# Self-attention with two of its weight products made once on chip, and the key squares summed on ScalarE

## The reference, cut to what matters

```
x1 = layernorm(x + self_attention(x))
x2 = layernorm(x1 + cross_attention(x1, ctx))
y  = layernorm(x2 + mixture_of_experts(x2))

self_attention(x):                      # one head, 256 wide, causal
    n = (x - mean) / sqrt(var + 1e-5) * gamma + beta
    q, k, v = n @ qkv[:, :256], n @ qkv[:, 256:512], n @ qkv[:, 512:]
    p = softmax(mask(q @ k.T / 16))
    return (p @ v) @ o_proj + x

cross_attention: 16 query heads of 128, 4 key heads; q = n @ Wq + bq, k = ctx @ Wk + bk, each head
    divided by its root mean square (rmsnorm: mean(k*k) over 128, eps 1e-6) before the scores
```

## Time and profile before

| | us |
|---|---|
| median of 3 executions | 1892.0 (1889.64 to 1893.38) |
| the profiled execution, its own time | 1891.63 |
| span of that profile | 1889.9 |
| attention phase in that span | 0 to about 1158 |
| granted TensorE clock over the span | 0.925 of full speed |

### The profile page before, as it was taken

The page is one execution under the profiler, slowest core; times in us unless marked ns, Lnnn a source line. Parts: engine busy times, 40 slices in busy tenths (PEclk is TensorE's granted clock), DMA queues, the critical chain, the costliest instruction groups (busy, mean ns, idle before and its releaser), DMA issues. The chain is left out here.

```text
span 1889.9 us, 34753 instructions
## 1 busy us (share of the span) xinstructions
PE 1547.4 (82%) x9744; PEld 1255.8 (66%) x9744; DVE 1265.1 (67%) x3827; ACT 688.6 (36%) x1526; POOL 1050.4 (56%) x1023
## 2 busy tenths in 40 slices
PE   4799998999899898989999864777777878787685
PEld 3687877778788787777878753555555656555453
DVE  3688877877778887888888844345555555433486
ACT  3344444343443343434344411222232222222353
POOL 3457666666566666666666742445555545555321
PEclk7799999999999999999999976889999898988799
DMA  7323231222212111121111295655565655554496
GB/s 244 118 91 104 73 106 62 94 82 89 89 62 95 63 59 67 45 75 47 66 59 52 81 277 157 182 165 160 162 182 161 181 160 172 172 167 129 169 417 278
DMA packets 182979, 246.41 MB, mean 130 GB/s; under 512 B 30972, under 2 KB 159561, under 8 KB 178388
## 3 DMA queue, kind: packets, MB, share of 16 engines
q1 hardware_dynamic: 149188, 169.71, 28.7%
q0 software_dynamic: 27648, 69.28, 10.0%
q10 hardware_dynamic: 6032, 6.13, 0.9%
HBM read 136.19 MB, written 117.19 MB: 134 GB/s over the span
## 5 line engine op out<-in xcount | busy, mean ns | idle before, releaser
L1555 POOL DMA_INDIRECT expert_out_scratch<-y,target x320 | 318.7, 996 | 296.6 <-DVE y L1779 196.0
L558 POOL DMA_INDIRECT slot_scratch<-xrow x256 | 258.7, 1010 | 188.6 <-DVE xrow L1174 117.1
L598 PE MATMUL bank_c<-wq_w,x1t 128*128 128x512 f32 x768 | 215.4, 433 | 62.9 <-DVE q_work L1016 53.7
L598 PEld LDWEIGHTS bank_c<-wq_w,x1t 128*128 128x128 f32 x768 | 154.6, 209 | 113.1 <-DVE q_work L1016 67.8
L1614 PE MATMUL bank_g<-gu,x_turned 128*128 (+1 forms) x1408 | 217.1, 303 | 14.9 <-issue 12.4
L503 POOL TENSOR_TENSOR q_rs<-q_ve,minus_half 128x8 f32<-128x8 f32 x64 | 137.4, 2147 | 146.6 <-DVE q_ve L1005 142.9
L1614 PEld LDWEIGHTS bank_g<-gu,x_turned 128*128 128x128 f32 x1408 | 194.4, 214 | 31.0 <-issue 30.5
L1633 PE MATMUL bank_y<-dp,inter_t 64*128 (+1 forms) x352 | 137.2, 473 | 85.2 <-DVE y L1779 60.0
L1671 ACT ACTIVATE x_turned<-bank_x 128x512 f32<-128x512 f32 x176 | 105.3, 598 | 272.8 <-PE bank_x L1596 161.1
L1770 DVE TENSOR_TENSOR inter<-silu,bank_g 128x128 f32<-128x128 f32 x176 | 50.2, 285 | 220.1 <-ACT silu L1678 144.7
L744 PE MATMUL bank_d<-wo_w,o2t 128*128 128x256 f32 x1536 | 194.5, 287 | 2.0 <-DVE o2t L933 2.0
(11 more groups left out here) (240 smaller groups left out, 3305.3 us busy)
## 6 DMA issues: line engine op xcount, KB each, us to landing
x_rows<-slot_scratch SPq DMA_DIRECT2D x320, 136.0 KB
results<-expert_out_scratch SPq DMA_DIRECT2D x32, 1024.0 KB, 10.1
slot_scratch<-zeros SPq DMA_DIRECT2D x16, 816.0 KB, 4.2
dp<-in_down SPq DMA_DIRECT2D x161, 64.0 KB
slot_scratch<-zeros SPq DMA_DIRECT2D x8, 1088.0 KB, 9.4
gu<-in_gate_up SPq DMA_DIRECT2D x11, 768.0 KB
expert_out_scratch<-y,target POOLq DMA_INDIRECT x320
token_row_scratch<-xrow SPq DMA_DIRECT2D x32, 136.0 KB
```

Of the source, the lines that this page charges most:

```text
L558: nc.gpsimd.indirect_dma_start(out=slot_d[:, :], out_offset=bass.IndirectOffsetOnAxis(ap=xrow[slot][:, SLOT8 + k:SLOT8 + k + 1].bitcast(U3 ...
L598: last = nc.tensor.matmul(target, left[a][:, c, :], right(b, c), start=(n == 0 and c == 0), stop=(n == len(PASSES) - 1 and c == C - 1))
L1555: nc.gpsimd.indirect_dma_start(out=y_d[:, :], out_offset=bass.IndirectOffsetOnAxis(ap=target[n % 8][:, j:j + 1], axis=0), in_=y[s % 4][:, ...
```

## The change

Once, ahead of the loop (`fuse`), PE turns the three parts of qkv, multiplies Wq Wk^T and Wv Wo (the last with a factor 0.5), and the two products take the place of qkv in the three-pass format, 512 columns instead of 768. ACT issues its DMAs first, o_proj ahead of them, and then copies for `fuse`. Per tile, one product gives t = n Wq Wk^T and v' = 0.5 n Wv Wo. Only t is turned; the scores are t against the full-precision x_n turned, for which ACT keeps one more copy (xn_full). The exponentials are used undivided; p @ v' is one matmul that yields the output rows, and the reciprocal of the row sum comes in at `x1_add`. As v' is halved, x_res is added once and the layernorm's eps is LN_EPS / 4. `self_output`, `copy_v`, `copy_self_out` and p1n are gone. The key squares move from POOL to ACT, one Square per head with the engine's own row sum, and wait also for the key transposes of the tile before. Two waits of SP ahead of the last weight loads and the places of some tiles in memory are also changed. The order of DVE's step is not edited: the logits copy stands where it stood, in `route_choose` after `x_moments`.

```
@@ tensors
-        qkv_w = [sb(f"qkv_w{n}", [P, C, 3 * D], F32R) for n in (HI, LO)]
-        x_g, x_n, v = (sb(name, [P, D]) for name in ("x_g", "x_n", "v"))
+        qkv_w = [sb(f"qkv_w{n}", [P, C, 2 * D], F32R) for n in (HI, LO)]
+        x_g, x_n = (sb(name, [P, D]) for name in ("x_g", "x_n"))
         qk = sb("qk", [P, 2 * D])
+        v = qk[:, D:2 * D]
...
@@ SP
-                sp.wait_ge(sig["v_projected"], TILES)
-                sp.wait_ge(sig["q_projected"], 4 * TILES)
+                sp.wait_ge(sig["self_proj"], TILES)
+                sp.wait_ge(sig["q_biased"], 4 * TILES)
...
-                sp.wait_ge(sig["q_transposed"], 2 * TILES)
-                sp.wait_ge(sig["k_transposed"], TILES)
+                sp.wait_ge(sig["scored"], 2 * TILES)
@@ POOL
-            def square_keys(t):
-                pool.wait_ge(sig["k_biased"], t + 1)
-                nc.gpsimd.tensor_tensor(k2s[:, :, :], k2[:, :, :], k2[:, :, :], ALU.mult).then_inc(sig["k_squared"], 1)
...
-                at(c, square_keys)
@@ PE
-                product(bank_a[:, 1, :], xnt, lambda b, c: qkv_w[b][:, c, 0:2 * D]).then_inc(sig["qk_projected"], 1)
-                product(bank_a[:, 0, 0:D], xnt, lambda b, c: qkv_w[b][:, c, 2 * D:3 * D])\
-                    .then_inc(sig["v_projected"], 1)
+                product(bank_a[:, 1, :], xnt, lambda b, c: qkv_w[b][:, c, :]).then_inc(sig["qk_projected"], 1)
...
-                for c in range(2 * C):
+                for c in range(C):
...
-                    last = nc.tensor.matmul(bank_a[:, 1, 0:P], qkt[:, c, :], qkt[:, C + c, :], start=(c == 0),
+                    last = nc.tensor.matmul(bank_a[:, 1, 0:P], tt[:, c, :], xnf[:, c, :], start=(c == 0),
...
-                pe.wait_ge(sig["self_probs"], t + 1)
+                pe.wait_ge(sig["self_exp"], t + 1)
...
             def self_attend(t):
                 pe.wait_ge(sig["self_pt_copied"], t + 1)
-                for c in range(C):
-                    last = nc.tensor.matmul(bank_b[:, 0, c * P:(c + 1) * P], v[:, c * P:(c + 1) * P], p1t[:, :],
-                                            start=True, stop=True)
-                last.then_inc(sig["self_out"], 1)
+                nc.tensor.matmul(bank_b[:, 0, 0:D], p1t[:, :], v, start=True, stop=True).then_inc(sig["self_proj"], 1)
...
+            def fuse():
+                pe.wait_ge(sig["qkv_loaded"], 16)
+                for n, target in enumerate((bank_c[:, 0, :], bank_c[:, 1, :], bank_d[:, 0, :])):
+                    for k in range(C):
+                        for c in range(C):
+                            last = nc.tensor.transpose(target[:, k * D + c * P:k * D + (c + 1) * P],
+                                                       qkv_parts[:, c, n * D + k * P:n * D + (k + 1) * P], identity[:, :])
+                    last.then_inc(sig["fused_turned"], 1)
+                pe.wait_ge(sig["fused_copied"], 3)
+                pe.wait_ge(sig["o_loaded"], 16)
+                for c in range(C):
+                    for k in range(C):
+                        nc.tensor.matmul(bank_d[:, c, 0:D], turned[0][:, k, c * P:(c + 1) * P], turned[1][:, k, :],
+                                         start=(k == 0), stop=(k == C - 1))
+                    for k in range(C):
+                        last = nc.tensor.matmul(bank_d[:, c, D:2 * D], turned[2][:, k, c * P:(c + 1) * P], o_w[:, k, :],
+                                                start=(k == 0), stop=(k == C - 1))
+                last.then_inc(sig["fused_made"], 1)
@@ ACT
+            def square_keys(t):
+                act.wait_ge(sig["k_biased"], t + 1)
+                if not (isinstance(t, int) and t == 0):
+                    act.wait_ge(sig["k_transposed"], t)
+                for g in range(KV):
+                    last = nc.scalar.activation(k2s[:, g, :], k2[:, g, :], ACT.Square, accum_out=k2_ss[:, g:g + 1])
+                last.then_inc(sig["k_squared"], 1)
...
+                copy("xn_full", flat(xnf[:, :, :]), bank_a[:, 0, 0:D], "xn_transposed", t + 1)
...
                 at(d, cross_out_high, 0)
+                at(c, square_keys)
                 at(e, copy_x2)
                 at(c, copy_queries, 0)
-                at(b, copy_self_out)
@@ DVE
-                dve.wait_ge(sig["self_recip"], t + 1)
-                nc.vector.tensor_scalar_mul(p1n[:, :], p1[:, :], p1_rec[:, :]).then_inc(sig["self_probs"], 1)
...
-                nc.vector.scalar_tensor_tensor(h1[:, :], x_res[:, :], 2.0, bank_b[:, 0, 0:D], ALU.mult, ALU.add)\
+                dve.wait_ge(sig["self_recip"], t + 1)
+                nc.vector.scalar_tensor_tensor(h1[:, :], bank_b[:, 0, 0:D], p1_rec[:, :], x_res[:, :], ALU.mult, ALU.add)\
...
-                mean_square(k2s[:, :, :], k2_ss[:, :], k2_ve[:, :], "k", t + 1)
+                nc.vector.tensor_scalar(k2_ve[:, :], k2_ss[:, :], 1.0 / HD, RMS_EPS, ALU.mult, ALU.add)\
+                    .then_inc(sig["k_var"], 1)
```

More of the change, by code:

```diff
@@ L158, in attention_phase @@
         xnt = [sb(f"xnt{n}", [P, C, P], F32R) for n in (HI, LO)]
-        qkt = sb("qkt", [P, 2 * C, P])
-        s1, p1, p1n, p1t = (sb(name, [P, P]) for name in ("s1", "p1", "p1n", "p1t"))
-        o1t = sb("o1t", [P, C, P])
+        tt = sb("tt", [P, C, P])
+        xnf = sb("xn_full", [P, C, P])
+        s1, p1, p1t = (sb(name, [P, P]) for name in ("s1", "p1", "p1t"))
         x1t = [sb(f"x1t{n}", [P, C, P], F32R) for n in (HI, LO)]
@@ L167, in attention_phase @@
         k2s = sb("k2s", [P, KV, HD])
+        h1, x1 = (sb(name, [P, D]) for name in ("h1", "x1"))
+        k2t = sb("k2t", [P, KV, P])
         with nc.sbuf_tensor("wo_stage", [P, HEADS * D], F32) as wo_stage:
@@ L170, in attention_phase @@
         o2t = [sb(f"o2t{n}", [P, HEADS, P], F32R) for n in (HI, LO)]
+        with nc.sbuf_tensor("turned_home", [P, 3 * C * D], F32) as turned_home:
+            pass
         wo_w = [sb(f"wo_w{n}", [P, HEADS, D], F32R) for n in (HI, LO)]
@@ L272, in flat @@
             return a.rearrange("p a b -> p (a b)")
+        qkv_parts = qkv_stage.rearrange("p (c n) -> p c n", c=C)
+        turned = [turned_home[:, n * 2 * D:(n + 1) * 2 * D].rearrange("p (k n) -> p k n", k=C) for n in range(3)]
         half = HEADS // 2
-        SMALL = 9
+        SMALL = 8
         LAG = 5
@@ L632, in self_probs_transpose @@
             def self_probs_transpose(t):
-                pe.wait_ge(sig["self_probs"], t + 1)
+                pe.wait_ge(sig["self_exp"], t + 1)
                 pe.wait_ge(sig["x1_lo"], t)
-                nc.tensor.transpose(bank_b[:, 0, 0:P], p1n[:, :], identity[:, :]).then_inc(sig["self_pt"], 1)
+                nc.tensor.transpose(bank_b[:, 0, 0:P], p1[:, :], identity[:, :]).then_inc(sig["self_pt"], 1)
             def self_attend(t):
                 pe.wait_ge(sig["self_pt_copied"], t + 1)
-                for c in range(C):
-                    last = nc.tensor.matmul(bank_b[:, 0, c * P:(c + 1) * P], v[:, c * P:(c + 1) * P], p1t[:, :],
-                                            start=True, stop=True)
-                last.then_inc(sig["self_out"], 1)
-            def self_output(t):
-                if isinstance(t, int) and t == 0:
-                    pe.wait_ge(sig["small_loaded"], 16 * SMALL)
-                pe.wait_ge(sig["self_ot"], t + 1)
-                for c in range(C):
-                    last = nc.tensor.matmul(bank_b[:, 0, 0:D], o1t[:, c, :], o_w[:, c, :], start=(c == 0),
-                                            stop=(c == C - 1))
-                last.then_inc(sig["self_proj"], 1)
+                nc.tensor.matmul(bank_b[:, 0, 0:D], p1t[:, :], v, start=True, stop=True).then_inc(sig["self_proj"], 1)
             def x1_transpose(t):
@@ L777, in step @@
                 at(f, route_score)
-                at(c, self_output)
                 at(b, self_transpose)
@@ L939, in moments @@
                 dve.wait_ge(sig[name + "_moments"], n1)
-                nc.vector.tensor_scalar_add(ve[:, :], mv[:, 1:2], LN_EPS).then_inc(sig[name + "_var"], 1)
+                nc.vector.tensor_scalar_add(ve[:, :], mv[:, 1:2], eps).then_inc(sig[name + "_var"], 1)
             def normalise(done, target, source, mv, rs, name, n1):
```

38 lines of the change are left out of this document (17 added, 21 removed).

## The result

| | kernel before | changed kernel |
|---|---|---|
| median, us | 1890.74 (1882.45 to 1908.51, 20 runs) | 1906.22 (20 runs) |
| ratio | | 1.006, 95% interval 1.0033 to 1.0088 |
| profiled execution, own time | 1891.63 | 1906.85 |
| span of it | 1889.9 | 1905.1 |
| granted clock over the span | 0.925 | 0.915 |

The fastest run of the changed kernel took 1887.77 us. One of its 20 was disturbed (2304.82 us) and is left out of the ratio. By the ratio the change costs some 11 us (the two medians lie 15.5 apart): the forecast's range holds it, its word "no change" doesn't.

A forecast was written before the change was run, and what follows sets the result against it. The prediction took a ring through GpSimd's chain to the query scaling, 33 us per tile, as the bound. 1891.6 + 0 from engines + 0 from the key chain + 1 from the start = 1892.6, 1893 against the median; range 1848 to 1922.

The forecast's parts named there:

- no change: Whole kernel: 1893 us forecast against the median of 1892.0; as worked out, chance 0.53.
- TensorE's 2.4 us per tile, worth 0: TensorE's removed matmuls, mostly between first and second query transposes: 77 us over 32 tiles, hidden behind GpSimd's chain.
- the 1 to 2 that the text named: Sign of being right: TensorE waits 1 to 2 us per step at the second query transposes for GpSimd's query scaling.
- the ring: Loop: third query product, keys and values, GpSimd through query scaling, VectorE's chain, exponential, h, bias add set 33 us.
- VectorE's p1n and reduction, GpSimd's squares, worth 0: Loop: VectorE's removed work becomes waiting or idle time; GpSimd loses 1.03 us per tile, but key power can't start earlier.
- ScalarE's squares, shift 0: Behind the o2t copies: four squares take 1.63 us, key power 0.13 later or unshifted; taken as 0.
- The start, net +1: Before the loop: first product near 24 or 20.5 instead of 15.35, partly given back; net -1 to +2.5, taken +1.
- my two bounds: Start: 12 transposes about 3.6 us, a copy 0.6, 8 float32 matmuls 7.6 or 4.3 us.
- Rival C: TensorE idles 2 us more before the second query transposes, its clock falls each step: 25 us, 1918; chance 0.08.
- Rival A (TensorE later than its records): TensorE carries its load to h, so removed work shortens steps: half gives 1855, all 1818; chance 0.25.
- The unnamed wait of h: VectorE's h waits 3.21 us until 541.35 for a release the profile can't name; the row against the ring.
- dearer squares: Between o2t copies and k_ve: 0.59 instead of 0.38 us a square, +0.86 per tile, 27 us, 1920; chance 0.14.

The follow-up runs named there:

- experiment 1: Changed kernel with the old value projection's 256-column product put back on TensorE in every tile, its result unread: 1896.17 us, ratio 1.0025.
- experiment 11: Changed kernel; ScalarE squares keys earlier and scales them; small loads and key/value weight rounding moved into its wait for the fused product: 1847.77 us, chip C, ratio 0.9767.
- experiment 12: Kernel before, old self-attention kept, with ScalarE squaring the keys ahead of its values copy and scaling them: 1860.07 us on chip C, ratio 0.9835.
- experiment 6: Changed kernel with ScalarE squaring the keys ahead of its values copy and scaling them instead of GpSimd: 1593.82 us on chip B, ratio 0.9739.
- experiment 4: Kernel before with only the key squares moved to ScalarE, its own self-attention kept: 1885.90 us, ratio 0.9974.
- experiment 3: Changed kernel with ScalarE's loads of biases, mask, norms and router issued after its rounding of the fused weights: 1899.75 us, ratio 1.0048.
- experiment 2: Changed kernel with key squares back on GpSimd and their sums on VectorE: 1905.77 us, ratio 1.0069.
- experiment 9: Changed kernel unedited, run as a control on chip C: 1898.38 us, ratio 1.0049 to the kernel before.
- experiment 8: Changed kernel with four unread products in TensorE's two waits of the step without a next tile: 1652.89 us on chip B, ratio 1.0100.
- experiment 10: Changed kernel with small loads and key/value weight rounding in ScalarE's fused-product wait, plus unread TensorE products in the last step: 1892.53 us, chip C, ratio 1.0025.

## Why the prediction was right or wrong

**TensorE's 2.4 us per tile, worth 0: right, in a size that was too large.** They became the wait ahead of the second query transposes, 1.2 us, inside the 1 to 2 that the text named, and giving the v product back cost nothing in the pitch (experiment 1). The size was too large. In part this is `self_attend`, for which I had 0.17 us less: it took 0.71 before and takes 0.70. The rest I put down to the records of neighbouring groups, which overlap, so that their times can't simply be added. The stretch from 300 to 900 us, some 18 steps, before:

```profile
300.00:900.00 600.00, 539.29 (x3570) 465.37 (x3569) 482.95 (x1143) 247.15 (x482) 388.58 (x360) 0.97 0.21 73
```

and after:

```profile
300.00:900.00 600.00, 518.68 (x3355) 437.92 (x3356) 471.57 (x1113) 256.89 (x611) 371.86 (x341) 0.97 0.22 73
```

TensorE's busy time fell by 20.6, 1.1 us per step and not 2.4. With the ring shortened they are worth some 0.33 per tile (experiments 11 and 12).

**The ring through GpSimd's chain: right.** Lengthened by 1.9 us it costs 3.45 per step, shortened by two small moves it gives 1.5 to 1.6 (both on chip B). VectorE's mask ends 0.08 behind L532 again, drawn out to 1.12 us; in experiment 6, where GpSimd idles at one such moment (562.09), the same instruction takes 0.23 us. The Trainium skill (SBUF — State Buffer, "SBUF: two separate sides") calls the port pair that VectorE and GpSimd share an exclusive lock: "the other fully blocks". The rows agree.

**VectorE's p1n and reduction, GpSimd's squares, worth 0: right within what can be measured**; p1n was not tested alone, and for the squares see the next part.

**ScalarE's squares, shift 0: a quarter of a microsecond too high.** One follows the next at 0.295 us (558.29, 558.59, 558.88, 559.17), the four with reads take 1.28; I had 1.63 or less, from an exponential that reads a bias. The key power stands 0.33 behind the second query power, since squares start only at 558.29. Counted from the o2t copy it comes 0.24 us sooner than before. If every step took that over, it would be 7 us; experiment 4 found 5 (0 to 10).

**The start, net +1: too small.** Measured +7.1 at the first query product, where I had -1 to +2.5, and +3.0 and +3.2 at tile 1; the text's own sign of being wrong, a first query product later than 46 us, came true (49.87). The step of the working that failed is the sentence that ScalarE's DMA issues move ahead of ScalarE's rounding, "where it waits for qkv anyway". I priced the issuing engine and forgot the landing: the weights came 4.4 to 4.8 us late, and with the loads behind them they did not (experiment 3). The transposes and products took 14.34 to 23.9, inside my two bounds. So the first product was at 26.68, not at 20.5 to 24. Of the 7.1 us, the landing accounts for 4.8 and leaves 2.3, inside my range; some 4 of the 7.1 are gone again by tile 1.

**The last step: missing.** Rival C had the mechanism, more idle in front of L691 (now L674) and a clock that falls, but spread over 31 steps at 0.8 us. In the loop's steady part the clock is the same as before (0.97 over 300 to 900 us in both); TensorE's self product stands between the waits there. In the one step that has no self product it fell in all five profiles on the slower chips that have the fused weights, the old chain on GpSimd and no idle products, and that cost 6 us; it fell in none of the four there that have the old self-attention or the idle products. With the shorter chain (experiment 11) the clock fell for some 3 us only and the step took 29.0. I took the cover away in the mean step and didn't ask about the step at the end of the pipeline. Yet my evidence against rival C was that very step: the stretch from 1053 to 1060 in the earlier trace rows, idle 2.9 of 7 us at full clock, is the one without a next tile, with `self_output` in it. The changed kernel is idle 3.0 of the same 7 us, and its clock there is 0.78.

**Rival A (TensorE later than its records): fell.** Experiment 1 gives TensorE the v product back for nothing. The unnamed wait of h on which the rival stood is absent on chip B, with the same matmuls.

**Sum.** Start +3, last step +6: 9 us of the measured 11 (1.0060) or 9 (1.0049). The two halves by themselves fit roughly: the fused weights alone cost 13 us (experiment 2, start +4.3 and last step +5.6), the squares alone give 5 (experiment 4). The other 10 us by which the first two profiles differ behind the last key power I don't attribute: there the same kernel has 814.8 us in its first profile and 800.1 in experiment 9, and from the end of the attention phase on, ten profiles on the slower chips, all with the same code there, take between 725 and 740 us.

**How much was luck.** That the loop's step would stay was reasoned, and it held. That the total stayed in the range was in part luck: one term of the sum was a third of its measured size, one was missing, and the range was wide for other reasons, a faster TensorE and dearer squares, neither of which came.

## What to carry to other kernels

Work taken from the busiest engine is worth nothing while that engine stands once per turn for another; find the chain that it stands for, and move an instruction of it to an idle engine (1.7% on chip C, from two small moves to ScalarE in the kernel before; 2.3% there together with the change and its mended start). Look at the first and last turns of a pipeline by themselves: an instruction removed there may have been what kept TensorE's clock up, or what kept loads out of each other's way. And weigh a DMA moved forward by what lands later for it, not only by the queue that issues it.

## What the runs showed that I had not expected

**Chips differ.** The kernel before took some 1890 us on two chips and 1636 on B. A part lies in the loop: with the change 33.0 us per step on the slower ones and 30.9 on B. On the slower chips h follows over 3 us of VectorE idling in some steps (5 of 20 between 300 and 960 us in the changed kernel's first profile, 3 in the kernel before's), on chip B in none. The changed kernel's first profile, with GpSimd's last indirect DMA of its burst of six and VectorE's h:

```profile
545.15 0.98 POOL L557 DMA_INDIRECT slot_scratch<-xrow  x1 [0.30 <-issue]
...
547.34 0.42 DVE L1077 TENSOR_TENSOR h<-x_res,bank_d 128x256 f32<-128x256 f32 x1 [3.25 <-remote]
```

Chip B, experiment 8:

```profile
545.26 0.98 POOL L557 DMA_INDIRECT slot_scratch<-xrow  x1 [0.30 <-issue]
...
545.70 0.42 DVE L1084 TENSOR_TENSOR h<-x_res,bank_d 128x256 f32<-128x256 f32 x1 [0.24 <-PE bank_d L732]
```

In that first profile h began some 1.2 us behind the end of the burst in all five of these steps. In the step shown of chip B it starts in the middle of the burst. What releases it the trace doesn't name, and no run here tells it; it stays open, as does the rest of the difference between the chips, most of which lies in the expert phase (some 730 us against 555).

**Idle products can pay.** Eight records of matmuls without a reader, 2 us of TensorE's time, saved 6.5 us (experiment 10). The Trainium skill (TensorE: Matmul & The Clock Gate, "What's actually happening") has the throttled state as the default that activity releases; by that rule such products should help, and the clock of 1.00 instead of 0.50 agrees.
